# The chosen rows of a routed ffn: a gather by matmul against an indexed send through DRAM

## The chip, the core and the metric

The kernel runs on one core of a Trainium2 chip. Its time is the device time of one execution in microseconds (us); three executions of the kernel before are given. The engines are TensorE (PE, with its weight loads shown apart as PEld), VectorE (DVE), ScalarE (ACT), GpSimd (POOL) and SyncE (SP), which only issues transfers. All data are float32.

## What is computed

The input x has 64 samples of 256 rows and 256 columns. Two layers follow each other, each made of a graph attention block and an ffn block, and each block is added to what goes in. The change is in the ffn of layer 0, a routed one: every row gets a weight, the 127 rows of the greatest weight are taken out, go through a two-layer ffn, are scaled by their weight and are put back in their places.

```python
def _L0_ffn_ref(x, attention_mask, wr, br, w1, b1, w2, b2):
    weights = (jnp.einsum('bsd,do->bso', x, wr) + br)[..., 0]
    k = max(1, int(CAPACITY * s))
    kk = k - 1 if k > 1 else 1
    _, idx = jax.lax.top_k(weights, k)
    sel_idx = idx[:, :kk]
    sel = jnp.take_along_axis(x, sel_idx[:, :, None], axis=1)
    h = jax.nn.gelu(jnp.einsum('bkd,dh->bkh', sel, w1) + b1)
    y = jnp.einsum('bkh,hd->bkd', h, w2) + b2
    w_sel = jnp.take_along_axis(weights, sel_idx, axis=1)
    y = y * w_sel[..., None]
    batch_idx = jnp.arange(b)[:, None]
    processed = jnp.zeros_like(x).at[batch_idx, sel_idx].set(y)
    return processed + x
...
x = x + _L0_gnn_ref(_layernorm(x, axis=-1), ...)
x = x + _L0_ffn_ref(_layernorm(x, axis=-1), ...)
x = x + _L1_gnn_ref(_layernorm(x, axis=-1), ...)
x = x + _L1_ffn_ref(_layernorm(x, axis=-1), ...)
```

## The kernel before

The kernel works one sample at a time, but as a pipeline over samples. A sample's work is cut into some fifty steps, whose names begin with the block: `a_` and `b_` for the first attention block and its two stages, `q_` for the routed ffn, `g_` for the second attention block, `m_` for the last ffn (a Mamba block). The table STEPS gives each engine an order of steps, written out by hand, and each step has a lag: in turn t the engine does the step for sample t minus lag. All weights stay in SBUF. An engine does its steps strictly in the order of its list, and every step waits on semaphores for what it needs. There are 70 turns; in the first and the last few only some of the steps have a sample, the middle ones are one hardware loop in which every step has one.

A tile of 256 rows lies in SBUF as 128 partitions by two blocks (U = 2). The steps around the change, in the order in which a sample passes through them:

- `q_norm` (DVE, L819): the normalised rows `xn["q"]`.
- `q_route` (DVE, PE, ACT): the weight of each row, as a column `wcol` and as a row `wrow`.
- `q_rank` (DVE, L966): each row's rank is the number of rows with a greater weight (L971). From the ranks it makes `pick`, a matrix of 256 by 128 zeros and ones: a 1 where the row's rank is the slot's number (L978). Slot 127 holds -1, so only ranks 0 to 126 find a place.
- `q_gather` (PE, L1298): transposes `pick` into bank Q0 (two transposes, L1302, wanted later for the way out), and multiplies `xn["q"]` with `pick` (L1305), which gives the chosen rows already transposed. On ACT, `q_gather` copies both to SBUF as `pickT` and `selT` (L645, L646).
- `q_ffn1`, `q_gelu`, `q_ffn2` (PE, ACT, DVE), and `q_scatter` (PE, L1329), which puts the results back in their rows by a product with `pickT`.

On PE the steps `m_da`, `a_turn`, `g_att`, `b_pturn` stand just ahead of `q_gather`, and `b_att`, `m_cum_col`, `q_ffn1.0` just behind. `b_att` (L1284 with output A) needs `pT_b`, which ACT copies out of PSUM in its `b_pturn` (L608). ACT's own order there is `g_att` (L616, it waits for PE's `g_att`), `b_pturn` (L608), `g_elu` (L632), `q_gather` (L645, L646).

On POOL the step `m_dt_log` is a chain of thirteen tiny instructions (L458 to L470), each waiting for the one before, then `dt` (L478) and `m_da` (L483, L484). Its last instruction lets PE's `m_da` (L1379, the transposes of dA) go. SP issues in each turn the loads of two copies of a sample (L351, L360), the store of the result (L371), and a store and a spread of the cumulated sums through a DRAM scratch (L365, L367).

Of the kernel before, what the change touches and what calls it, by code (L numbers as in the profile page):

```python
# [7 lines left out]
ALU = mybir.AluOpType  # L8
ACT = mybir.ActivationFunctionType
F32 = mybir.dt.float32  # L10
I32 = mybir.dt.int32
AX_X = mybir.AxisListType.X

P = 128
# [30 lines left out]
def gnn_ffn_mamba_kernel(nc, x, adj, mlp1_w, mlp1_b, mlp2_w, mlp2_b, W_fc, a_fc, W_hand, a_hand,  # L45
# [24 lines left out]
    with ExitStack() as ctx:  # L70
        def sb(name, shape, dt=F32):
            return ctx.enter_context(nc.sbuf_tensor(name, shape, dt))
# [98 lines left out]
        pick = sb("pick", [P, U, P])  # L171
        pickT = sb("pickT", [P, N])
# [37 lines left out]
        cum_dram = nc.dram_tensor("cum_dram", [NH, N], F32, kind="Internal").ap()  # L210

# [8 lines left out]
        def rows1(half, u, extra=0):  # L220
# [13 lines left out]
            wsum_ready w_ps wrow_ready rank_ready pick_ready sel_ps sel_ready  # L234
# [11 lines left out]
        out_stored = sem("out_stored")  # L246

# [68 lines left out]
        def _(sp):  # L316
# [56 lines left out]
            turns(sp, "sync", dict(a_load=a_load, a_residual=a_residual, m_spread=m_spread, m_store=m_store), {})  # L373
# [4 lines left out]
        def _(pool):  # L378
            def constants():
# [34 lines left out]
                pool.wait_ge(PL, 5)  # L414

# [78 lines left out]
            def m_rms(b):  # L494
# [5 lines left out]
                q_turn=q_turn,  # L500
                m_turn=m_turn, m_dt_log=m_dt_log, m_da=m_da, m_xrow=m_xrow,
# [230 lines left out]
        def _(v):  # L732
# [233 lines left out]
            def q_rank(b):  # L966

                v.wait_ge(S["wrow_ready"], b)
                spare = gsq[:, :, :].rearrange("p (a c) r -> p a (c r)", a=4)
                for u in range(U):  # L970
                    last = nc.vector.scalar_tensor_tensor(out=spare[:, u, :], in0=wrow[:], scalar=wcol[:, u:u + 1],  # L971
                                                          in1=tie_gap[:, u, :], op0=ALU.subtract, op1=ALU.is_ge,
                                                          accum_out=rank[:, u:u + 1])
                last.then_inc(S["rank_ready"], 1)
                v.wait_ge(S["rank_ready"], b)

                for u in range(U):
                    last = nc.vector.tensor_scalar(pick[:, u, :], slot[:], rank[:, u:u + 1], None, ALU.is_equal)  # L978
                last.then_inc(S["pick_ready"], 1)
# [147 lines left out]
        def _(pe):  # L1127
# [341 lines left out]
```

## Time and profile before

| what | value |
|---|---|
| median of 3 executions | 3751.22 us (3750.86 to 3752.01) |
| the profiled execution, its own time | 3752.41 us |
| span of its profile, first to last instruction | 3750.7 us |
| PE busy | 3618.9 us, 96% |
| DVE busy | 2973.1 us, 79% |
| ACT busy | 2364.2 us, 63% |
| POOL busy | 993.9 us, 26% |
| mean granted clock of TensorE | 0.985 of 2.4 GHz |
| moved by DMA | 126.85 MB |

The span is the time between the first and the last instruction in the profile; 1.7 us of the execution lie around it. Busy time counts neither waits nor the issue of transfers. The ends of matmuls are modelled in the profile and overlap with the next matmul's start, so that PE's rows overlap in time, and a short wait of PE can hide under such an end. PEld shows when the weights (the stationary operand) of a matmul are loaded, which happens ahead of the matmul and needs the operand to be there. A float32 matmul of the program is two rows of the trace; a transpose is one.

### The profile page before, as it was taken

Reading aid. Unit: us, or ns where it says so; the run is one execution under the profiler, and the core shown is the slowest. Engines: PE = TensorE matmul, PEld = TensorE weight load, DVE = VectorE, ACT = ScalarE, POOL = GpSimd, SP = SyncE. Lnnn points to the kernel's source line nnn. Section 1 sums busy time; section 2 is a strip of 40 time slices with the busy share of each in tenths; the row PEclk is TensorE's granted clock in tenths of the full one; section 3 lists DMA queues with packets and bytes.
Section 4 is the critical chain, followed back from the end, with each engine's and each line's share of the span. In section 5 each row is a group of like instructions: output and inputs, shape, how many; then the busy total and the mean of one; then the engine's idle time right before and its main releaser. Section 6 shows DMA issues by size and latency. Waiting matters only on the chain.

```text
span 3750.7 us, 63924 instructions
## 1 busy us (share of the span) xinstructions
PE 3618.9 (96%) x21016; PEld 3158.1 (84%) x21016; DVE 2973.1 (79%) x7729; ACT 2364.2 (63%) x5314; POOL 993.9 (26%) x1821
## 2 busy tenths in 40 slices
PE   6799999999999999999999999999999999999975
PEld 4688888888888888888888888888888888888864
DVE  3468878878888888888888888888887887888875
ACT  2356666667666666666666666666666666666654
POOL 0022232232232232232222223223223223223222
PEclk8899999999999999999999999999999999999998
DMA  3000100100100110110010010010010010010000
GB/s 102 12 26 32 39 28 31 39 28 31 39 28 31 39 36 23 39 39 23 36 39 28 31 39 28 31 39 28 31 39 28 31 39 28 31 39 29 30 29 31
DMA packets 73763, 126.85 MB, mean 34 GB/s; under 512 B 9984, under 2 KB 64128, under 8 KB 65536
## 3 DMA queue, kind: packets, MB, share of 16 engines
q1 hardware_dynamic: 69360, 126.39, 9.8%
q10 hardware_dynamic: 4368, 0.03, 0.1%
q8 instruction: 18, 0.29, 0.0%
q14 instruction: 17, 0.14, 0.0%
HBM read 109.10 MB, written 17.30 MB: 34 GB/s over the span
## 4 chain that ended last, share of the span: by engine, by line
PE 87%; DVE 8%; issue 2%; ACT 1%; POOL 0%; ACTq 0%; DVEq 0%; POOLq 0%
PE A L1199 12%; PE M L1335 7%; PE A L1219 7%; PE Q L1323 6%; PE A L1237 6%; PE A L1188 6%; PE Q L1316 6%; PE M L1369 6%; PE M L1428 6%; PE A L1284 3%; PE A L1246 3%; PE Q L1246 3%; PE Q L1284 3%; PE A L1229 2%; PE M L1357 2%
## 5 line engine op out<-in xcount | busy, mean ns | idle before, releaser
L1199 PE MATMUL A<-w_fc,o1T 128*128 128x256 f32 (+1 forms) x2048 | 454.7, 380 | 3.8 <-ACT o1T L541 3.8
L1199 PEld LDWEIGHTS A<-w_fc,o1T 128*128 128x128 f32 x2048 | 382.9, 189 | 57.8 <-ACT o1T L541 4.0
L433 POOL TENSOR_TENSOR var_m<-mv_m,epsilon 128x2 f32<-128x2 f32 x64 | 12.6, 197 | 1414.7 <-DVE mv_m L813 1414.7
L710 ACT ACTIVATE dec<-cumB,cumcol 128x256 f32<-128x256 f32 (+1 forms) x1024 | 366.2, 443 | 0.0
L1022 DVE SCALAR_TENSOR_TENSOR acc<-M,w_conv,acc 128x255 f32<-128x255 f32 (+2 forms) x768 | 315.0, 470 | 0.0
L1335 PE MATMUL M<-xT_m,w_in 128*128 128x256 f32 x1280 | 297.5, 379 | 0.8 <-DVE tz L1064 0.5
L1219 PE MATMUL A<-h,low 128*128 128x257 f32 (+1 forms) x1024 | 256.4, 395 | 22.9 <-DVE low L854 14.0
L1335 PEld LDWEIGHTS M<-xT_m,w_in 128*128 128x128 f32 x1280 | 237.7, 190 | 32.1 <-DVE tz L1064 2.0
L1323 PE MATMUL Q<-w_down,gsq 128*128 128x256 f32 x1024 | 241.2, 390 | 9.7 <-DVE gsq L995 9.7
L1316 PE MATMUL Q<-selT,w_up 128*128 128x128 f32 x2048 | 249.5, 275 | 0.9 <-ACT selT L646 0.9
L1064 DVE SCALAR_TENSOR_TENSOR tz<-tz,M 128x512 f32<-128x512 f32 x128 | 88.1, 688 | 202.5 <-ACT tz L693 202.5
L1188 PE MATMUL A<-xT_a,w_mlp 128*128 128x256 f32 x1024 | 236.1, 384 | 8.3 <-ACT xT_a L533 5.1
L1237 PE MATMUL A<-e,w_mlp 128*128 128x256 f32 x1024 | 241.0, 389 | 0.7 <-DVE e L878 0.7
L1219 PEld LDWEIGHTS A<-h,low 128*128 128x128 f32 x1024 | 189.1, 194 | 61.5 <-DVE low L854 38.6
L1316 PEld LDWEIGHTS Q<-selT,w_up 128*128 128x128 f32 x2048 | 238.8, 192 | 1.2 <-ACT selT L646 1.1
L1428 PE MATMUL M<-w_comb,xr 128*128 128x256 f32 x1024 | 231.6, 379 | 3.4 <-DVE xr L1085 3.4
L1323 PEld LDWEIGHTS Q<-w_down,gsq 128*128 128x128 f32 x1024 | 193.5, 194 | 47.1 <-DVE gsq L995 22.2
L1369 PE MATMUL M<-xT_m,w_in 128*128 128x256 f32 x1024 | 231.7, 379 | 0.0
L658 ACT ACTIVATE acc<-M,c_conv,w_conv 128x256 f32<-128x256 f32 x320 | 168.4, 567 | 92.1 <-PE M L1335 92.1
L490 POOL TENSOR_TENSOR xdt<-xr,dt 128x1024 f32<-128x1024 f32 x64 | 129.4, 2022 | 366.2 <-ACT xr L699 366.2
L1072 DVE TENSOR_TENSOR dec<-dec,cb 128x2048 f32<-128x2048 f32 (+1 forms) x128 | 223.8, 1749 | 1.7 <-ACT dec L714 1.6
L1188 PEld LDWEIGHTS A<-xT_a,w_mlp 128*128 128x128 f32 x1024 | 192.6, 193 | 33.6 <-issue 9.0
(235 smaller groups left out, 8830.3 us busy)
## 6 DMA issues: line engine op xcount, KB each, us to landing
cumB<-cum_dram SPq DMA_DIRECT2D x64, 1024.0 KB, 4.7
x_in<-in_x SPq DMA_DIRECT2D x64, 256.0 KB, 2.8
x<-in_x SPq DMA_DIRECT2D x64, 256.0 KB, 2.9
out<-x3b SPq DMA_DIRECT2D x64, 256.0 KB, 2.8
w_mlp<-in_L_gnn_mlp_w SPq DMA_DIRECT2D x2, 512.0 KB, 6.3
w_fc<-in_L_gnn_W_fc SPq DMA_DIRECT2D x2, 512.0 KB, 8.6
w_up<-in_L_ffn_w SPq DMA_DIRECT2D x1, 1024.0 KB, 11.7
w_down<-in_L_ffn_w SPq DMA_DIRECT2D x1, 1024.0 KB, 12.9
```

The lines of the kernel that those rows point to most:

```text
L710: last = nc.scalar.activation(dec[:, h, :], columns[:, h, :], ACT.Relu, bias=cumcol[:, i, h:h + 1], scale=-1.0)
L1022: last = nc.vector.scalar_tensor_tensor(out=acc[:, k, late:], in0=src, scalar=w_conv[:, k, tap:tap + 1], in1=acc[:, k, late:], op0=ALU.mul ...
L1188: last = nc.tensor.matmul(ps[:, (m - m0) * N:(m - m0 + 1) * N], w_mlp1[:, k, m * P:(m + 1) * P], xT["a"][:, k, :], start=(k == 0), stop=(k ...
L1199: last = nc.tensor.matmul(rows1(half, u, 2), o1T[:, k, u * P:(u + 1) * P], w_fc[:, k, half, 0:D + 2 * i], start=(k == 0), stop=(k == KH - 1))
L1219: last = nc.tensor.matmul(rows1(half, u, 1), p1[:, j, u * P:(u + 1) * P], h1[:, j, half, 0:D + 1 - half], start=(j == 0), stop=(j == U - 1))
L1237: last = nc.tensor.matmul(A1[:, m * N:(m + 1) * N], w_mlp2[:, k, m * P:(m + 1) * P], z1T[:, k, :], start=(k == 0), stop=(k == KH - 1))
L1246: last = nc.tensor.matmul(banks[u][:, 0:D + 2], src[:, c, u * P:(u + 1) * P], w[:, c, :], start=(c == 0), stop=(c == KD - 1))
L1316: last = nc.tensor.matmul(ps[:, (m - m0) * P:(m - m0 + 1) * P], w_up[:, c, m * P:(m + 1) * P], selT[:, c, :], start=(c == 0), stop=(c == K ...
L1323: last = nc.tensor.matmul(Q0[:, 0:D], gl[:, m, :], w_down[:, m, :], start=(m == 0), stop=(m == KF - 1))
L1335: last = nc.tensor.matmul(ps[:, at:at + N], w_in[:, c, X0 + k * P:X0 + (k + 1) * P], xT["m"][:, c, :], start=(c == 0), stop=(c == KD - 1))
L1369: last = nc.tensor.matmul(ps[:, (k - 2 * i) * N:(k - 2 * i + 1) * N], w_in[:, c, Z0 + k * P:Z0 + (k + 1) * P], xT["m"][:, c, :], start=(c ...
L1428: last = nc.tensor.matmul(M2[:, u * D:(u + 1) * D], yg[:, c, u * P:(u + 1) * P], w_comb[:, c, :], start=(c == 0), stop=(c == KI - 1))
```

## The change

PE no longer multiplies with `pick` to gather. In its place:

- DVE computes `place` after the ranks, 128 by 2 whole numbers: the rank, plus one where the rank is 127 or more. Row 127 of the scratch is so never written by a sample.
- POOL sends `xn["q"]` to a DRAM scratch `sel_dram` of 257 rows, row by row to the row named by `place`. That is one indirect DMA for each of the two blocks, 128 rows of 1 KB each, in a new step `q_send`. It stands in the middle of `m_dt_log`, which is cut in two: its first two instructions before `q_send`, the other eleven behind.
- SP reads the first 128 rows of the scratch back into `sel` when both sends have landed, in a new step `q_sel` between `m_store` and `m_spread`.
- PE's `q_gather` keeps the two transposes of `pick`, waits for the read, and transposes `sel` (two transposes) where it had four matmuls.
- Once, at the start, POOL writes a row of zeros into row 127 of the scratch and waits for it.
- DVE's `q_norm` and `q_rank` each wait for the sends of the sample before.

```diff
-    "gpsimd": [('a_norm', 0), ('q_norm', 2), ('g_norm', 3), ('q_turn', 2), ('m_rms', 5), ('m_dt_log', 4), ('m_da', 4), ('m_turn', 4), ('m_norm', 3), ('m_xrow', 4)],
-    "sync": [('a_load', 0), ('a_residual', 2), ('m_store', 6), ('m_spread', 5)],
...
+    "gpsimd": [
+        ("a_norm", 0), ("q_norm", 2), ("g_norm", 3), ("q_turn", 2), ("m_rms", 5), ("m_dt_log.0", 4), ("q_send", 2),
+        ("m_dt_log.1", 4), ("m_da", 4), ("m_turn", 4), ("m_norm", 3), ("m_xrow", 4),
+    ],
+    "sync": [
+        ("a_load", 0), ("a_residual", 2), ("m_store", 6), ("q_sel", 3), ("m_spread", 5),
+    ],
...
+            def q_sel(b):
+
+                sp.wait_ge(sel_sent, 32 * b)
+                sp.dma_start(sel[:], sel_dram[0:P, :]).then_inc(sel_back, 16)
...
+                nc.gpsimd.dma_start(sel_dram[TOPK:TOPK + 1, :], tie_gap[0:1, 0, :]).then_inc(unused_row, 16)
+                pool.wait_ge(unused_row, 16)
...
+            def q_send(b):
+
+                after(S["place_ready"], b)
+                before(pool, S["sel_ps"], b)
+                pool.nop(nofuse=True)
+                for u in range(U):
+                    nc.gpsimd.indirect_dma_start(sel_dram, bass.IndirectOffsetOnAxis(place[:, u:u + 1], 0),
+                                                 xn["q"][:, u, :], None).then_inc(sel_sent, 16)
...
-                for i, link in enumerate(links):
+                for i in ((0, 1), range(2, CHAIN))[half]:
...
+                    if k == "q" and not (isinstance(b, int) and b < 2):
+                        v.wait_ge(sel_sent, 32 * (b - 1))
...
-
+                if not (isinstance(b, int) and b < 2):
+                    v.wait_ge(sel_sent, 32 * (b - 1))
+                nc.vector.scalar_tensor_tensor(out=place[:], in0=rank[:], scalar=float(TOPK), in1=rank[:], op0=ALU.is_ge,
+                                               op1=ALU.add).then_inc(S["place_ready"], 1)
...
+                pe.wait_ge(sel_back, 16 * b)
                 for c in range(KD):
-                    for u in range(U):
-                        last = nc.tensor.matmul(Q0[:, N + c * P:N + (c + 1) * P], xn["q"][:, u, c * P:(c + 1) * P],
-                                                pick[:, u, :], start=(u == 0), stop=(u == U - 1))
+                    last = nc.tensor.transpose(Q0[:, N + c * P:N + (c + 1) * P], sel[:, c * P:(c + 1) * P], ident[:])
                 last.then_inc(S["sel_ps"], 1)
```

The order of all other steps is the same. On PE, at the head of the hardware loop, `q_gather` stood like this before:

```order
L1273 MATMUL A<-ident,sc_b 128x128 x4
L295 UNCONDITIONAL_BRANCH
L295 ISA
L1302 MATMUL Q<-ident,pick 128x128 x2
L1305 MATMUL Q<-pick,xn_q 128x128 x4
L1280 REGISTER_ALU
L1284 MATMUL A<-hp_b,pT_b 128x256 x4
```

And it stands like this in the change, where lines further down in the file have moved by some fifty:

```order
L1331 MATMUL A<-ident,sc_b 128x128 x4
L329 UNCONDITIONAL_BRANCH
L329 ISA
L1360 MATMUL Q<-ident,pick 128x128 x2
L1361 REGISTER_ALU
L1363 MATMUL Q<-ident,sel 128x128 x2
L1338 REGISTER_ALU
L1342 MATMUL A<-hp_b,pT_b 128x256 x4
```

The four matmuls of L1305 have become two transposes of `sel`; the step before and the step behind are the same. On POOL, in the same loop, `m_dt_log` began like this before (`dt_w` are its small tiles):

```order
L458 TENSOR_TENSOR dt_w<-dt_e,twos 128x16
L475 ISA
L459 TENSOR_TENSOR dt_w<-dt_w,inverse 128x16
L475 REGISTER_ALU
L460 TENSOR_TENSOR dt_w<-dt_e,dt_w 128x16
```

And like this in the change:

```order
L509 TENSOR_TENSOR dt_w<-dt_e,twos 128x16
L526 ISA
L510 TENSOR_TENSOR dt_w<-dt_w,inverse 128x16
L491 DMA sel_dram<-xn_q,place 257x256 x2
L526 REGISTER_ALU
L511 TENSOR_TENSOR dt_w<-dt_e,dt_w 128x16
```

Two sends now stand behind the second instruction of the chain, and the eleven instructions behind them, `dt` and `m_da` follow only then. On SP the loop now issues as follows; the read of `sel` is the new row between the store of the result and the two transfers of the cumulated sums:

```order
L410 DMA out<-x3b 128x2x256
L405 REGISTER_ALU
L406 DMA sel<-sel_dram 128x256
L398 REGISTER_ALU
L399 DMA cum_dram<-cumT 8x256
L400 REGISTER_ALU
L401 DMA cumB<-cum_dram 128x2048
```

Nothing else of SP's order has moved.

## Rows read from the trace of the kernel before

**Rows 1.** The page, busy time by engine and the chain that ended last

```profile
PE 3618.9 (96%) x21016; PEld 3158.1 (84%) x21016; DVE 2973.1 (79%) x7729; ACT 2364.2 (63%) x5314; POOL 993.9 (26%) x1821
...
PE 87%; DVE 8%; issue 2%; ACT 1%; POOL 0%; ACTq 0%; DVEq 0%; POOLq 0%
```

**Rows 2.** One turn in the middle: stretch, length, busy us (count), clock, DMA

```profile
2018.60:2074.40 55.80, 55.65 (x330) 48.81 (x328) 46.10 (x121) 36.87 (x84) 15.43 (x28) 1.00 0.10 33
```

**Rows 3.** Timeline of PE around q_gather: start us, length us, instruction, count

```profile
2015.33 1.89 PE L1284 MATMUL Q<-hp_g,pT_g 128*128 128x256 f32 x8
...
2017.50 0.38 PE L1302 MATMUL Q<-ident,pick 128*128 128x128 f32 x2
2017.72 1.06 PE L1305 MATMUL Q<-pick,xn_q 128*128 128x128 f32 x8
2018.64 1.99 PE L1284 MATMUL A<-hp_b,pT_b 128*128 128x256 f32 x8
```

**Rows 4.** Timeline of the weight loads in the same place

```profile
2014.46 0.30 PEld L1379 LDWEIGHTS M<-ident,dA 128*8 128x8 f32 x2
...
2017.61 0.97 PEld L1305 LDWEIGHTS Q<-pick,xn_q 128*128 128x128 f32 x8
2018.63 0.73 PEld L1284 LDWEIGHTS A<-hp_b,pT_b 128*128 128x128 f32 x4
```

**Rows 5.** Timeline of ACT there; in brackets the idle time before and its end

```profile
2017.26 0.84 ACT L616 ACTIVATE ea_g<-Q,rr_g 128x256 f32<-128x256 f32 x2 [0.39 <-PE Q L1284]
2017.99 0.59 ACT L608 COPY pT_b<-A 128x512 f32<-128x512 f32 x1
```

**Rows 6.** Timeline of DVE: the end of q_rank and what follows

```profile
2004.44 0.48 DVE L978 TENSOR_SCALAR pick<-slot,rank 128x128 f32<-128x128 f32 x2
2007.06 0.69 DVE L1064 SCALAR_TENSOR_TENSOR tz<-tz,M 128x512 f32<-128x512 f32 x1 [2.14 <-ACT tz L693]
```

**Rows 7.** Timeline of POOL in that turn

```profile
2002.67 2.91 POOL L459 TENSOR_TENSOR dt_w<-dt_w,inverse 128x16 f32<-128x16 f32 x1
...
2009.45 0.26 POOL L484 TENSOR_SCALAR dt<-dt 128x16 f32<-128x16 f32 x1
2009.68 1.27 POOL L448 TENSOR_TENSOR x3b<-x,c_lin 128x512 f32<-128x512 f32 x1
```

**Rows 8.** Timeline of SP in that turn, the store of the sums

```profile
2016.14 0.30 SPq L365 DMA_DIRECT2D cum_dram<-cumT  x1
```

**Rows 9.** The page, DMA issues: count, KB each, median us to landing

```profile
cumB<-cum_dram SPq DMA_DIRECT2D x64, 1024.0 KB, 4.7
x_in<-in_x SPq DMA_DIRECT2D x64, 256.0 KB, 2.8
```

**Rows 10.** Timeline of the start: issues of transfers and the first sample

```profile
3.05 1.44 ACTq L512 DMA_DIRECT2D c_conv<-in_L_ffn_conv_b  x1
...
5.77 0.20 POOL L433 TENSOR_TENSOR var_a<-mv_a,epsilon 128x2 f32<-128x2 f32 x1
...
7.68 1.09 PE L1177 MATMUL A<-ident,xn_a 128*128 128x128 f32 x4 [7.68 <-DVE xn_a L821]
...
11.88 1.28 ACT L533 ACT_TABLE_LOAD   x1 [11.88 <-issue]
12.10 4.34 SPq L335 DMA_DIRECT2D w_route<-in_L_ffn_wr  x1
```

**Rows 11.** Timeline of the first sample's gather

```profile
119.38 1.83 PEld L1305 LDWEIGHTS Q<-pick,xn_q 128*128 128x128 f32 x8
119.41 0.59 ACT L608 COPY pT_b<-A 128x512 f32<-128x512 f32 x1 [1.21 <-PE A L1273]
...
121.09 1.73 PEld L1284 LDWEIGHTS A<-hp_b,pT_b 128*128 128x128 f32 x8
```

**Rows 12.** Timeline of the last turn with a q_gather, POOL and PE

```profile
3627.09 0.26 POOL L484 TENSOR_SCALAR dt<-dt 128x16 f32<-128x16 f32 x1
...
3627.40 0.38 PE L1379 MATMUL M<-ident,dA 128*8 128x128 f32 x2
```

More of the change, by code:

```diff
@@ L11 @@
 I32 = mybir.dt.int32
+U32 = mybir.dt.uint32
 AX_X = mybir.AxisListType.X
@@ L29 @@
 STEPS = {
-    "tensor": [('q_gather', 3), ('b_att', 2), ('m_cum_col', 5), ('q_ffn1.0', 3), ('b_res', 2), ('q_ffn1.1', 3), ('a_mlp1.0', 1), ('a_mlp1.1', 1), ('m_xrow', 5), ('m_cb', 5), ('a_fc.0', 1), ('a_fc.1', 1), ('q_ffn2', 3), ('a_bcast', 1), ('m_turn', 4), ('q_scatter', 3), ('m_y.0', 5), ('m_y.1', 5), ('a_att.0', 1), ('g_turn', 3), ('a_att.1', 1), ('g_proj', 3), ('m_out', 5), ('g_bcast', 3), ('m_ss', 5), ('a_uturn', 1), ('m_dt', 4), ('q_route', 2), ('a_mlp2', 1), ('m_z', 4), ('g_pturn', 3), ('b_proj', 1), ('m_xbc_a', 4), ('b_bcast', 1), ('m_xbc_b', 4), ('m_da', 4), ('a_turn', 0), ('g_att', 3), ('b_pturn', 1)],
@@ L32 @@
-    "scalar": [('a_att', 1), ('m_gated', 5), ('a_elu_b', 1), ('g_proj', 3), ('q_route', 2), ('m_dt_exp', 4), ('g_exp', 3), ('a_mlp2', 1), ('m_z', 4), ('b_proj', 1), ('g_pturn', 3), ('m_xbc_a', 4), ('m_xbc_b', 4), ('b_exp', 1), ('g_att', 3), ('b_pturn', 1), ('g_elu', 3), ('q_gather', 2), ('b_att', 1), ('b_elu_b', 1), ('a_turn', 0), ('m_silu', 4), ('q_gelu_a', 2), ('a_mlp1', 0), ('m_decay.0', 4), ('q_gelu_c', 2), ('m_decay.1', 4), ('m_xrow', 4), ('a_factors', 0), ('a_fcol', 0), ('g_turn', 2), ('m_turn', 3)],
@@ L33 @@
-    "gpsimd": [('a_norm', 0), ('q_norm', 2), ('g_norm', 3), ('q_turn', 2), ('m_rms', 5), ('m_dt_log', 4), ('m_da', 4), ('m_turn', 4), ('m_norm', 3), ('m_xrow', 4)],
-    "sync": [('a_load', 0), ('a_residual', 2), ('m_store', 6), ('m_spread', 5)],
+    "tensor": [
+        ("q_gather", 3), ("b_att", 2), ("m_cum_col", 5), ("q_ffn1.0", 3), ("b_res", 2), ("q_ffn1.1", 3),
+        ("a_mlp1.0", 1), ("a_mlp1.1", 1), ("m_xrow", 5), ("m_cb", 5), ("a_fc.0", 1), ("a_fc.1", 1), ("q_ffn2", 3),
+        ("a_bcast", 1), ("m_turn", 4), ("q_scatter", 3), ("m_y.0", 5), ("m_y.1", 5), ("a_att.0", 1), ("g_turn", 3),
+        ("a_att.1", 1), ("g_proj", 3), ("m_out", 5), ("g_bcast", 3), ("m_ss", 5), ("a_uturn", 1), ("m_dt", 4),
+        ("q_route", 2), ("a_mlp2", 1), ("m_z", 4), ("g_pturn", 3), ("b_proj", 1), ("m_xbc_a", 4), ("b_bcast", 1),
+        ("m_xbc_b", 4), ("m_da", 4), ("a_turn", 0), ("g_att", 3), ("b_pturn", 1),
+    ],
@@ new lines @@
+    "vector": [
+        ("g_stats", 4), ("a_probs", 2), ("g_norm", 4), ("m_y.0", 6), ("a_att", 2), ("m_y.1", 6), ("q_norm", 3),
+        ("g_proj", 4), ("m_sq", 6), ("q_route", 3), ("a_elu_c", 2), ("g_mask", 4), ("m_ms", 6), ("a_uturn", 2),
+        ("g_lrelu", 4), ("m_dt", 5), ("a_norm", 1), ("g_max", 4), ("m_out", 6), ("q_rank", 3), ("m_gate", 5),
+        ("b_proj", 2), ("b_mask", 2), ("b_lrelu", 2), ("b_max", 2), ("g_pturn", 4), ("m_scan", 5), ("m_conv_b.0", 5),
+        ("b_pturn", 2), ("m_conv_b.1", 5), ("g_elu_b", 4), ("m_conv_b.2", 5), ("m_cum_col", 5), ("b_elu_c", 2),
+        ("b_x1", 2), ("q_gelu_a", 3), ("m_silu", 5), ("g_x3", 4), ("q_stats", 2), ("a_stats", 0), ("q_gelu_b", 3),
+        ("m_stats", 4), ("m_cb", 5), ("a_fc", 1), ("m_norm", 4), ("q_ffn2", 3), ("m_mix.0", 5), ("a_fcol", 1),
+        ("m_mix.1", 5), ("q_scatter", 3), ("a_maxima", 1), ("q_x2", 3),
+    ],
@@ new lines @@
+    "scalar": [
+        ("a_att", 1), ("m_gated", 5), ("a_elu_b", 1), ("g_proj", 3), ("q_route", 2), ("m_dt_exp", 4), ("g_exp", 3),
+        ("a_mlp2", 1), ("m_z", 4), ("b_proj", 1), ("g_pturn", 3), ("m_xbc_a", 4), ("m_xbc_b", 4), ("b_exp", 1),
+        ("g_att", 3), ("b_pturn", 1), ("g_elu", 3), ("q_gather", 2), ("b_att", 1), ("b_elu_b", 1), ("a_turn", 0),
+        ("m_silu", 4), ("q_gelu_a", 2), ("a_mlp1", 0), ("m_decay.0", 4), ("q_gelu_c", 2), ("m_decay.1", 4),
+        ("m_xrow", 4), ("a_factors", 0), ("a_fcol", 0), ("g_turn", 2), ("m_turn", 3),
+    ],
@@ L35 @@
+    "gpsimd": [
+        ("a_norm", 0), ("q_norm", 2), ("g_norm", 3), ("q_turn", 2), ("m_rms", 5), ("m_dt_log.0", 4), ("q_send", 2),
+        ("m_dt_log.1", 4), ("m_da", 4), ("m_turn", 4), ("m_norm", 3), ("m_xrow", 4),
+    ],
+    "sync": [
+        ("a_load", 0), ("a_residual", 2), ("m_store", 6), ("q_sel", 3), ("m_spread", 5),
+    ],
 }
@@ L171, in gnn_ffn_mamba_kernel @@
         pick = sb("pick", [P, U, P])
+        place = sb("place", [P, U], U32)
+        sel = sb("sel", [P, D])
         pickT = sb("pickT", [P, N])
@@ L210, in gnn_ffn_mamba_kernel @@
         cum_dram = nc.dram_tensor("cum_dram", [NH, N], F32, kind="Internal").ap()
+        sel_dram = nc.dram_tensor("sel_dram", [N + 1, D], F32, kind="Internal").ap()
         A0, A1, A2 = bank("A0"), bank("A1"), bank("A2")
@@ L246, in gnn_ffn_mamba_kernel @@
         out_stored = sem("out_stored")
+        sel_sent = sem("sel_sent")
+        sel_back = sem("sel_back")
+        unused_row = sem("unused_row")
         DV, PL, PEs, AC = [sem(f"setup{i}") for i in range(4)]
@@ L371, in m_store @@
                 sp.dma_start(out[b - 1].rearrange("(u p) d -> p u d", p=P), x4[:]).then_inc(out_stored, 16)
-            turns(sp, "sync", dict(a_load=a_load, a_residual=a_residual, m_spread=m_spread, m_store=m_store), {})
+            turns(sp, "sync", dict(a_load=a_load, a_residual=a_residual, m_spread=m_spread, q_sel=q_sel, m_store=m_store), {})
             sp.wait_ge(cum_stored, 16 * B)
@@ L451, in _, with m_dt_log @@
             CHAIN = 13
-            def m_dt_log(b):
-                after(S["dt_e_ready"], b)
+            def m_dt_log(b, half):
+                if half == 0:
+                    after(S["dt_e_ready"], b)
                 w = dt_w
@@ L472, in m_dt_log @@
                 assert len(links) == CHAIN
-                for i, link in enumerate(links):
+                for i in ((0, 1), range(2, CHAIN))[half]:
                     if i:
                         pool.wait_ge(S["dt_chain"], nth(b, CHAIN, i))
-                    link().then_inc(S["dt_chain"], 1)
+                    links[i]().then_inc(S["dt_chain"], 1)
+                if half == 0:
+                    return
                 after(S["dt_chain"], b * CHAIN)
@@ L499, in _ @@
                 a_norm=rstd_of("a"), q_norm=rstd_of("q"), g_norm=rstd_of("g"), m_norm=rstd_of("m"),
-                q_turn=q_turn,
-                m_turn=m_turn, m_dt_log=m_dt_log, m_da=m_da, m_xrow=m_xrow,
+                q_turn=q_turn, q_send=q_send,
+                m_turn=m_turn, **parts("m_dt_log", m_dt_log, 2), m_da=m_da, m_xrow=m_xrow,
                 m_rms=m_rms), dict(a_norm=constants, m_turn=first_m_turn, m_da=first_m_da))
```

3 lines of the change are left out of this document (1 added, 2 removed).

## The prediction

> **What bounds the kernel now.** I read the page first. PE is busy 96% of the span and 87% of the chain that ended last is PE's [rows 1]. One turn in the middle takes 55.80 us, PE is busy 55.65 us of it at a granted clock of 1.00 (2.4 GHz), DVE 46.10, ACT 36.87 and POOL 15.43 [rows 2]. By this view whatever is taken from PE comes off the time, and the change takes something from PE.
>
> The second view is the timeline around the step that changes. PE starts the transposes of `pick` at 2017.50, the gather's matmuls at 2017.72 and `b_att` at 2018.64 [rows 3]. PE's rows show no idle time there, but matmul ends are modelled: the gather's eight rows are given as 1.06 us and overlap `b_att`. So the third view is that of the weight loads. The eight of the gather take 0.97 us from 2017.61, the last one ending at 2018.58, and loads follow each other about 0.11 us apart ((2018.58 - 0.19 - 2017.61) / 7, where 0.19 is the length of one). The next would be due near 2018.50. The first of `b_att` starts at 2018.63 [rows 4]: it is held by about 0.13 us. What holds it is in the fourth view. ACT waits for PE's `g_att`, which ends at 2015.33 + 1.89 = 2017.22 [rows 3], works on `ea_g` from 2017.26, starts the copy `pT_b` at 2017.99 and ends it at 2017.99 + 0.59 = 2018.58 [rows 5]. `b_att` needs `pT_b`, and its load starts 0.05 us after that copy's end. **The start of `b_att` is thus set by `g_att` and two pieces of ACT's work, 1.41 us after `g_att`'s end, and not by the gather that stands between.** The reader is to see that a busy PE row covers this, and that the weight load gives it away.
>
> **What the change removes.** The four matmuls are eight rows from 2017.72 to 2018.64: 0.92 us, 0.115 each [rows 3]. In their place stand two transposes, priced by the two of `pick`: 2017.50 to 2017.72, 0.22 us [rows 3]. That is 0.70 us less work of PE in each of 64 turns, 45 us. But in the middle turns PE comes to `b_att` 0.70 us sooner and waits until 2018.63 as before, since neither `g_att`, `ea_g` nor `pT_b` has moved. The 0.13 us of waiting becomes 0.83, the turn stays 55.80, and the gain is 0. Behind `b_att` nothing is sooner, for PE is in order. The clock: 0.8 us of idle in 55.80 leaves PE busy 98%; I put nothing for it.
>
> In the first sample it is otherwise. The weight loads of the gather run from 119.38 to 121.09, 1.71 us at the lower clock of that stretch (0.21 each); `pT_b` is ready at 119.41 + 0.59 = 120.00 [rows 11]. Two transposes take 0.43 in place of 1.71, so `b_att` could start 1.28 sooner, at 119.81, and is held until 120.05: I put a gain of 1.2 us with the tail of the pipeline. The other turns at the ends can give at most 0.70 each; I put 0.
>
> **What the change adds: the sends on POOL.** The trace has no DMA issued by POOL. Call G the time for which the two sends hold POOL. They stand behind the second instruction of the chain, which ends at 2002.67 + 2.91 = 2005.58 [rows 7]; `place` is there by then (`pick` starts at 2004.44 [rows 6], and `place` stands ahead of it). Queued behind them are eleven links, `dt` and `m_da`, which end at 2009.45 + 0.26 = 2009.71 [rows 7] and would end at 2009.71 + G. PE's `m_da` waits for them; its first weight load starts at 2014.46 [rows 4]. The cover is 4.75 us, and PE's work ahead (`m_z`, `m_xbc`) is what gives it. Up to G = 4.75 the sends cost nothing; beyond, `m_da` is late, `g_att` behind it is late by the same, and so is `b_att`: each us over costs one us in each of about 60 turns. `x3b`, further back on POOL, ends at 2010.95 [rows 7] and is wanted only by the next turn's `m_out`.
>
> G from below: two issues at 0.30, the shortest row of SP, 0.60 [rows 8]. From above: two at 4.34, the longest issue in the trace, 8.7 [rows 10]. I take two at 1.44, G = 2.9: the row of a load of many small pieces on ACT's queue [rows 10], nearest in kind to 128 rows with an address each.
>
> In the last turn with a gather the cover is gone: `dA` is ready at 3627.09 + 0.26 = 3627.35 and PE's `m_da` starts at 3627.40 [rows 12], so there the cost is G - 0.05 = 2.85 us, once (0.55 to 8.65).
>
> **The way through DRAM.** The sends leave POOL at 2005.58 + 2.9 = 2008.5. A send carries 128 KB and the read brings 128 KB back. Loads of 256 KB land 2.8 us after their issue, of 1024 KB 4.7 [rows 9]; I take 2.8 each for the last send and the read: 2008.5 + 5.6 = 2014.1. PE asks for `sel` at 2017.72 [rows 3], and since `b_att` is held anyway, a `sel` at 2018.4 still costs nothing. The cover is 3.6 to 4.3 us; with 4.7 twice it is 2017.9, still in time. In the last turn the sends start at 3623.2 (POOL's chain ends 4.13 us before `dA`) and `sel` is back at 3631.7, while PE asks at about 3632.4, since `m_da` is late by 2.85: nothing more.
>
> **Further waits.** SP's wait for the sends blocks the store of the sums, at 2016.14 [rows 8], 5 us after it would end (2011.3). On DVE `place` is a short instruction ahead of `pick`, and DVE idles 2.14 us behind it [rows 6]: 0. DVE's waits for the sends of the sample before look back a turn: 0. At the start POOL waits for one row to reach DRAM, from 5.77 on [rows 10], 2.8 us by the loads. The first sample's transposes, 7.68 to 8.77, would end 2.8 later, at 11.6, but ACT can't copy them before its table load ends at 11.88 + 1.28 = 13.16 [rows 10]: 0, with a cover of 4.4 us. If the first send of a run takes longer than the cover, I allow 3 us.
>
> **The sum** against the profiled execution: 3752.41 + 0 (middle turns) - 1.2 (first sample) + 2.85 (last turn) = 3754.1. The median of the runs is 1.19 below that execution: 3752.9, say 3753. Its own bounds: G = 0.60 and 0.70 at two turns of the ends give 3751.2 + 0.55 - 1.2 - 1.4 = 3749; G = 4.75 and 3 us at the start give 3751.2 + 4.7 - 1.2 + 3 = 3758. A measurement of this kernel can tell about 0.2%, 7.5 us, from no change.
>
> **The rivals.** *PE is the bound at this place and each turn gets shorter.* For it: the chain is 87% PE's, and PE shows 0.15 us idle a turn [rows 1, 2]. Against it: the weight load that starts 0.05 us behind `pT_b` [rows 4, 5]. It would give 62 middle turns x 0.70 = 43.4 less: 3753 - 43 = 3710. Chance 0.10.
>
> *The sends are longer than their cover* (the other side). The place is PE's `m_da`, the point from which it decides G = 4.75. With two sends of 3 us, G = 6, it gives 60 x 1.25 = 75, and 3 more in the last turn: 3831. For it: nothing in the trace shows what such a send costs, and POOL needs 2.91 us for one power of 16 columns [rows 7]. Against it: the middle of the issue rows is half of the cover. Chance 0.18, most of it between 3759 and 3831.
>
> *POOL works through the indices one after the other*, so that a send costs as much as the longest issue, 4.34 [rows 10]: G = 8.7, 60 x 3.95 = 237, and 5.8 more in the last turn, 3996 or more. POOL's power, 0.18 us a column by 2.91 / 16 [rows 7], shows that its software can be as slow. Chance 0.05. The Trainium skill has a rule for this, GPSIMD Engine Reference, section Performance pitfalls for Q7 kernels: a small read command, such as one per gather index, costs about 102 cycles that don't overlap. At the 1.2 GHz of its section Specifications, an estimate from that page is 128 x 102 cycles = 10.9 us a send, and the sum by it would be over 4700; no row here shows it.
>
> *The rows come back late.* Landings of more than 4.7 us each put `sel` behind 2018.4; each us over costs about 62. At 5.7 each it is 3753 + 62 x 1.5 = 3846. Chance 0.03.
>
> **Chances.** Forecast, no change that can be told, 0.64; faster 0.10; the three slower ones 0.26. The forecast's own range is 3749 to 3758. To leave out no more than 0.2 (the faster rival, the one index after the other, the late landing and the far end of the long sends) the range reaches to G = 6: 3749 to 3831.
>
> **What the new profile would show.** Right: a turn of 55.80, the first weight load of `b_att` 0.05 us behind `pT_b`'s end and over 0.7 us behind the load before it, PE's `m_da` where it was before `g_att`, the read of `sel` landed before PE's transposes of `pick`, and a later `m_da` only in the last turn. Wrong: PE waiting for `dt` or dA on POOL in every turn (the sends are too long), PE waiting for `sel` (the way is), or a turn near 55.1 (the hold by `pT_b` isn't one).

## The result and the profile after

| what | before | with the change |
|---|---|---|
| median of 20 executions each, side by side | 3752.11 us (3749.96 to 3753.18) | 3758.82 us (3756.01 to 3761.78) |
| ratio | | 1.0019, 95% interval 1.0012 to 1.0026 |
| the profiled execution | 3752.41 us | 3761.53 us |
| its span | 3750.7 us | 3759.8 us |

The change made the kernel 6.7 us slower. That is under the 7.5 us which the prediction took as the limit of what can be told, but the interval of the ratio lies above 1, so the small loss is real. The forecast was 3753. The profiled execution lies 2.7 us above its median, so of the 9.1 us by which the two spans differ some belongs to that one execution.

The page of the kernel after, against [rows 1]:

```profile
PE 3589.2 (95%) x20632; PEld 3114.3 (83%) x20632; DVE 2977.2 (79%) x7793; ACT 2364.9 (63%) x5314; POOL 1124.7 (30%) x1950
PE 84%; DVE 9%; issue 3%; ACT 3%; POOL 1%; DMA 0%; DVEq 0%; POOLq 0%
```

PE has 29.7 us less to do and POOL 130.8 us more, and neither shows in the time. One middle turn, from `b_att` to `b_att`, against [rows 2]:

```profile
2020.72:2076.52 55.80, 55.12 (x323) 48.08 (x323) 46.17 (x122) 36.89 (x84) 17.45 (x30) 1.00 0.11 38
```

The length is the same, 55.80, with PE busy 0.53 us less. The weight loads at the place of the change, against [rows 4], and then ACT, against [rows 5] (L1342 was L1284, L661 was L608, L669 was L616):

```profile
2019.48 0.25 PEld L1360 LDWEIGHTS Q<-ident,pick 128*128 128x128 f32 x2
2019.70 0.25 PEld L1363 LDWEIGHTS Q<-ident,sel 128*128 128x128 f32 x2
2020.72 1.59 PEld L1342 LDWEIGHTS A<-hp_b,pT_b 128*128 128x128 f32 x8 [0.77 <-ACT pT_b L661]
```

```profile
2019.36 0.84 ACT L669 ACTIVATE ea_g<-Q,rr_g 128x256 f32<-128x256 f32 x2 [0.39 <-PE Q L1342]
2020.09 0.59 ACT L661 COPY pT_b<-A 128x512 f32<-128x512 f32 x1
```

`pT_b` ends at 2020.68, the load of `b_att` follows 0.04 us later, and what were 0.13 us of hidden waiting are now 0.77, with a releaser named. The chain that was read out of three views before stands in one row now, because the gather no longer covers it. Summed over the kernel, in the view of all waits (total us, times, longest):

```profile
PEld A L1342 <- ACT pT_b L661: 48.5, 64, 1.1
```

POOL in the same turn, against [rows 7], and SP's read of `sel`:

```profile
2004.76 2.91 POOL L510 TENSOR_TENSOR dt_w<-dt_w,inverse 128x16 f32<-128x16 f32 x1
2007.86 1.07 POOL L491 DMA_INDIRECT sel_dram<-xn_q,place  x1 [0.18 <-issue]
2009.23 0.97 POOL L491 DMA_INDIRECT sel_dram<-xn_q,place  x1 [0.30 <-issue]
2010.23 0.23 POOL L511 TENSOR_TENSOR dt_w<-dt_e,dt_w 128x16 f32<-128x16 f32 x1
...
2014.02 0.26 POOL L537 TENSOR_SCALAR dt<-dt 128x16 f32<-128x16 f32 x1
```

```profile
2011.65 0.34 SPq L406 DMA_DIRECT2D sel<-sel_dram  x1
```

From the end of L510 (2007.67) to L511 are 2.56 us where the chain's links stand 0.07 to 0.08 apart: G is 2.5 us (2.9 forecast). POOL ends at 2014.28, and the first load of PE's `m_da` starts at 2016.56: 2.28 of the 4.75 us of cover are left. The page gives the two ways through DRAM, in KB where known and median us to landing:

```profile
sel<-sel_dram SPq DMA_DIRECT2D x64, 128.0 KB, 2.0
sel_dram<-xn_q,place POOLq DMA_INDIRECT x128, 2.5
```

`sel` is back at 2011.65 + 2.0 = 2013.65, and PE asks at 2019.8.

**Where the 9.1 us are.** I put the two traces beside each other by the start of the two `pick` transposes, once in each sample. The changed kernel is 2.69 us late at the first one, 2.28 two turns on. Over the middle turns it makes up 0.3 (55.794 a turn for 55.800), then loses 1.1 in one turn, 3.96 in the last turn with a gather, and 2.05 behind it: 2.69 - 0.41 - 0.3 + 1.1 + 3.96 + 2.05 = 9.1.

*The start*, against [rows 10], on POOL, on the chain that ended last, and the first sample's copy on ACT:

```profile
6.01 0.77 POOL L454 DMA_DIRECT2D sel_dram<-tie_gap  x1 [0.31 <-POOL slot L452]
12.39 0.20 POOL L474 TENSOR_TENSOR var_a<-mv_a,epsilon 128x2 f32<-128x2 f32 x1 [5.61 <-DMA sel_dram<-tie_gap]
```

```profile
6.01 6.29 DMA sel_dram<-tie_gap
```

```profile
15.42 0.59 ACT L586 COPY xT_a<-A 128x512 f32<-128x512 f32 x1 [2.44 <-PE A L1235]
```

One row of 1 KB took 6.29 us to land, not 2.8. The first sample's statistics stand behind it, its transposes on PE start at 14.30 for 7.68, 6.62 later. ACT's table load covered the first 4.4: the copy starts at 15.42 for 13.17, 2.25 later. The other 0.4 us come behind the copy. One part has a row, PE's wait for `low`, a preparation that DVE does behind the second sample's statistics; these start at 20.68 for 13.18, because the second load of `x_in` went out only when the first sample's rows were read:

```profile
27.49 3.75 PE L1257 MATMUL A<-w_fc,o1T 128*128 128x258 f32 x16 [0.24 <-DVE low L796]
```

The rest differs from one execution to the next. The copy is 2.08 to 2.34 us later in each of the five kernels with this wait, but their sixteen matmuls of `a_mlp1` behind it take 5.41 to 6.38 us. The kernel of "The sends alone" below, whose steps are those of the changed kernel up to the first gather, has that gather at 120.21, where the changed kernel has 121.85.

*The last turn with a gather*, against [rows 12]. PE:

```profile
3632.77 0.49 PE L1436 MATMUL M<-ident,dA 128*8 128x128 f32 x2 [2.58 <-POOL dt L537]
3633.05 3.51 PE L1342 MATMUL Q<-hp_g,pT_g 128*128 128x256 f32 x8
```

PE waits 2.58 us for POOL, and `g_att` behind it takes 3.51 us for the 1.89 of [rows 3]. The windows show why (the columns of [rows 2]):

```profile
3633.05:3636.40 3.35, 3.35 (x10) 2.55 (x9) 3.07 (x8) 0.00 (x0) 0.90 (x1) 0.51 0.12 27
3640.00:3700.00 60.00, 38.22 (x198) 31.20 (x196) 39.00 (x84) 32.53 (x67) 13.34 (x25) 0.81 0.07 23
```

The granted clock is 0.51, the lower level of 1.2 GHz, right behind that idle stretch. In the drain it is 0.81 from 3640 to 3700; the kernel before has 0.88 in the 60 us at the same distance behind its last gather. This second difference does not follow from the stop. Four kernels have the same last turn, with PE idle for 2.58 or 2.59 us and `g_att` at 3.41 to 3.57. In the changed kernel and in that of "The sends alone" the drain runs at 0.81, and the tail, from the last gather to the end, takes 123.4 and 123.3 us. In the one with the zero row waited for later and in the one of "Moving PE's waiting work" the drain runs at 0.87 and the tail takes 120.6 and 120.9, less than the 121.34 of the kernel before. What sets the clock of the drain is open, and so is what the 2.05 us are due to.

*The one longer turn* (56.90 us). POOL, then PE:

```profile
3235.35 1.07 POOL L491 DMA_INDIRECT sel_dram<-xn_q,place  x1 [0.18 <-issue]
3239.72 0.98 POOL L491 DMA_INDIRECT sel_dram<-xn_q,place  x1 [3.30 <-issue]
```

```profile
3245.38 0.38 PE L1436 MATMUL M<-ident,dA 128*8 128x128 f32 x2 [0.95 <-POOL dt L537]
```

Between the two sends are 3.30 us of issue, 0.30 elsewhere. G is 5.5 there, over the cover of 4.75, and one link of the chain takes 0.69 for 0.22; PE waits 0.95. The gap stands between the 113th and the 114th send of the kernel.

### The profile page after: what moved, and what is told of

Same layout as the page of the kernel before. It is cut to its first block, busy times and chain, and to the rows that moved or that the text cites. A ratio compares the mean times of both kernels' runs of the same rounds, so it can differ in the third digit from the quotient of the medians.

```text
span 3759.8 us, 63718 instructions
## 1 busy us (share of the span) xinstructions
PE 3589.2 (95%) x20632; PEld 3114.3 (83%) x20632; DVE 2977.2 (79%) x7793; ACT 2364.9 (63%) x5314; POOL 1124.7 (30%) x1950
## 4 chain that ended last, share of the span: by engine, by line
PE 84%; DVE 9%; issue 3%; ACT 3%; POOL 1%; DMA 0%; DVEq 0%; POOLq 0%
PE A L1257 12%; PE M L1392 7%; PE A L1277 6%; PE Q L1380 6%; PE A L1295 6%; PE Q L1373 6%; PE A L1246 6%; PE M L1426 6%; PE M L1485 6%; PE A L1342 3%; PE A L1304 3%; PE Q L1342 3%; PE Q L1304 3%; PE A L1287 2%; PE M L1414 1%
## 5 line engine op out<-in xcount | busy, mean ns | idle before, releaser
L1485 PEld LDWEIGHTS M<-w_comb,xr 128*128 128x128 f32 x1024 | 194.0, 190 | 30.7 <-DVE xr L1143 3.9
```

The costliest lines, as they stand in the source:

```text
L1485: last = nc.tensor.matmul(M2[:, u * D:(u + 1) * D], yg[:, c, u * P:(u + 1) * P], w_comb[:, c, :], start=(c == 0), stop=(c == KI - 1))
```

## The experiments

Each ran beside the kernel before, whose medians were 3751.28, 3751.63 and 3751.88 in the three sets. "Turn" is the median distance of two gathers in the trace. Theory A, the prediction's: `b_att` is held by `pT_b`, so that PE's saved time is lost, and the sends hide in their cover. The rivals: PE is the bound, or the sends are paid in every turn. What two kernels of different sets differ by is told from their medians as they stand; the medians of the kernel before differ by up to 0.8 us between the sets (that of the result had 3752.11).

### PE's part alone

The kernel before, with two transposes in place of the four matmuls and nothing sent. They transpose half of `xn["q"]` instead of choosing rows.

```diff
-                    for u in range(U):
-                        last = nc.tensor.matmul(..., xn["q"][:, u, c * P:(c + 1) * P], pick[:, u, :], ...)
+                    last = nc.tensor.transpose(..., xn["q"][:, 0, c * P:(c + 1) * P], ident[:])
```

> The kernel before, in which PE's gather is cut to the two transposes of the change (of a block of the normalised rows, so the rows that reach the ffn are not the chosen ones); no sends, no scratch, no read. Held by pT_b: the middle turn stays 55.80 us, b_att's first weight load starts 0.05 us behind pT_b's end, and the time is that of before less about 1 us of the first sample, 3751. PE is the bound there: 62 turns of 55.10, 3709.

Measured: 3751.45 (3750.1 to 3752.67), ratio 0.9999 (0.999 to 1.0008), turn 55.79.

```profile
2017.78 1.59 PEld L1284 LDWEIGHTS A<-hp_b,pT_b 128*128 128x128 f32 x8 [0.77 <-ACT pT_b L608]
```

The saved 0.70 us are gone without any send or wait for `sel`. The rival that PE is the bound here is refuted.

### The sends alone

The changed kernel with everything sent and read back, but PE gathers by its four matmuls, behind the wait for `sel`.

> The changed kernel with all its sends, reads and waits, in which PE gathers by its four matmuls as before. Held by pT_b: PE's 0.70 us are free in a middle turn, the turn is 55.80, and the time is that of the change plus 0.6 us of the first sample, 3759. PE is the bound and the sends ate its gain: 62 x 0.70 us more than the change, 3802.

Measured: 3760.36 (3758.93 to 3762.25), ratio 1.0023 (1.0014 to 1.0032), turn 55.79. The loss of the change is that of the sends and the start; none of it is a loss in every turn.

### Twice as many sends

Each send is done a second time, to a scratch that nobody reads, and the waits for the sends count twice as far.

```diff
                     nc.gpsimd.indirect_dma_start(sel_dram, ..., xn["q"][:, u, :], None).then_inc(sel_sent, 16)
+                    nc.gpsimd.indirect_dma_start(spare_dram, ..., xn["q"][:, u, :], None).then_inc(sel_sent, 16)
```

> The changed kernel with each send done twice, the second time to another scratch that nobody reads. Cover by PE's m_da: the sends hold POOL 5.1 us in place of 2.5, dA is ready 0.3 us behind the time at which PE wants it, 0.3 to 0.4 us in each of 60 turns and 2.6 in the last: 3780 to 3785, with PE waiting for POOL in every turn. If POOL's time is hidden whatever it is: 3759 to 3762. If each us of POOL costs a us of the turn: 3915.

Measured: 3799.59 (3798.61 to 3800.95), ratio 1.013 (1.0114 to 1.0145), turn 56.30. POOL is held 5.0 us. The PE row of a middle turn:

```profile
2036.39 0.38 PE L1439 MATMUL M<-ident,dA 128*8 128x128 f32 x2 [0.35 <-POOL dt L540]
```

The cover ends where the prediction put it: 0.25 us beyond 4.75, and POOL's `dA` took 0.59 where it takes 0.22 else, together 0.6, and the turn is 0.50 longer. That is 30 us. The rest over the expectation are two odd turns (60.66 and 61.97 for 56.30, 10 us) and the last turn (55.28 for 49.53, 5.8; the expectation allowed 2.6 for it). Both odd turns have the long gap:

```profile
1689.16 0.98 POOL L494 DMA_INDIRECT spare_dram<-xn_q,place  x1 [3.30 <-issue]
...
3271.16 0.96 POOL L492 DMA_INDIRECT sel_dram<-xn_q,place  x1 [3.27 <-issue]
```

The first stands behind the 113th send, the second behind the 226th. In each of the nine kernels with two sends a turn there is one such gap, behind the 113th send, at 3225 to 3240 us; here the same count is reached at 1689. So the gap goes by the number of sends and not by the turn or the time. What POOL does in it no row shows.

### The ends: the zero row, the last turn

```diff
-                pool.wait_ge(unused_row, 16)
...
+                if isinstance(b, int) and b == 1:
+                    pool.wait_ge(unused_row, 16)
```

The wait moves from the start to the first sends, some 100 us later.

> The changed kernel, in which POOL waits for the row of zeros only ahead of the first send and not before the first sample. The wait at the start is what the first turns lost: the first gather comes 2.7 us or a little more sooner, and the time is 3 us below the change, 3756. If something else of the send's first use costs the time (code, the first indirect send): 3759, the loss only moves.

Measured: 3754.68 (3753.6 to 3759.16), ratio 1.0011 (1.0002 to 1.002). The first gather is at 117.01 (121.85 in the changed kernel, 119.16 before), so more than the 2.69 comes back. The wait is not what the other 2.15 are due to: the first sample's copy on ACT starts at 13.07, as before the change, and the sixteen matmuls of `a_mlp1` behind it take 5.12 us for 6.18. Why they do is open.

In the second kernel the last sample neither sends nor reads, and PE gathers by matmul for it:

```diff
+                if isinstance(b, int) and b == B:
+                    return
```

> The changed kernel, in which the last sample alone is gathered by the four matmuls as before, with no send and no read for it. If the last turn's loss is POOL's sends ahead of the chain for dA: that turn is 49.5 us as before in place of 53.5, the clock doesn't fall behind it, and the time is 4 to 6 us below the change, 3753 to 3755. If the loss is the way through DRAM or the tail's own: 3759.

Measured: 3754.31 (3753.26 to 3755.54), ratio 1.0007 (0.9998 to 1.0016); last turn 49.34, tail 121.17. PE no longer waits there, and the matmuls keep the upper clock:

```profile
3629.67 1.89 PE L1346 MATMUL Q<-hp_g,pT_g 128*128 128x256 f32 x8
```

Each end is worth some 4 us by the medians, 4.1 and 4.5 (3.3 and 4.0 if each is taken against the kernel before of its own set). For the last turn that is what the turn itself gives, 4.15 us. Then both in one kernel:

> The changed kernel with both losses at the ends taken out: the wait for the zero row stands ahead of the first sends, and the last turn gathers by matmul without sends. Middle turns 55.79, first gather near 117.1, last turn 49.5 and no lower clock behind it. From the changed kernel's 3758.8 this takes 4.1 and 4.5 us: 3750 to 3751. If the two losses share a cause or one is made up in the drain, 3753 or more.

Measured: 3753.30 (3750.27 to 3759.31), ratio 1.0005 (0.9996 to 1.0014). Together they gave 5.5, not 8.6. In the profiled execution the last turn is 50.26 and the tail 122.41, 2.2 over the last kernel, which is of the size of the shortfall. Two windows of 40 us in the drain, of this kernel and then of the one before it, whose last gather is 2.2 us later:

```profile
3640.00:3680.00 40.00, 30.23 (x152) 24.14 (x150) 23.17 (x54) 18.14 (x40) 12.36 (x23) 0.85 0.05 19
```

```profile
3640.00:3680.00 40.00, 30.86 (x162) 24.77 (x160) 23.76 (x53) 19.84 (x45) 12.40 (x23) 0.91 0.02 8
```

The granted clock is 0.85 for 0.91. PE had not stopped ahead of the last gather in either, so here too the clock of the drain differs without such a stop. What decides it was not isolated, and so a microsecond or two of each end stays open.

### Moving PE's waiting work ahead of b_att

If `b_att` is held 0.77 us and PE has other work ready, the work can fill the hold: `m_cum_col` (2 transposes) and `b_res` (4) are 0.66 us. In the changed kernel:

```diff
-        ("q_gather", 3), ("b_att", 2), ("m_cum_col", 5), ("q_ffn1.0", 3), ("b_res", 2), ("q_ffn1.1", 3),
+        ("q_gather", 3), ("b_res", 2), ("m_cum_col", 5), ("b_att", 2), ("q_ffn1.0", 3), ("q_ffn1.1", 3),
```

> The changed kernel, in which PE does the residual's transposes (b_res, 0.44 us) and those of the sums (m_cum_col, 0.22 us) ahead of b_att in place of behind it. Held by pT_b: 0.66 of the 0.83 us in which PE waits are filled, the middle turn becomes 55.14, and the time is 40 us below that of the change, 3719. If the wait ahead of b_att is not on the path that sets the turn: 3759, as the change.

Measured: 3757.66 (3756.51 to 3759.03), ratio 1.0017 (1.0008 to 1.0026), turn 55.78. A miss by 39 us. The hold before `b_att` is filled, and another has opened 6 us on; PEld, then DVE:

```profile
2018.44 1.59 PEld L1342 LDWEIGHTS A<-hp_b,pT_b 128*128 128x128 f32 x8
2020.06 3.76 PEld L1373 LDWEIGHTS Q<-selT,w_up 128*128 128x128 f32 x32
2024.39 1.59 PEld L1246 LDWEIGHTS A<-xT_a,w_mlp 128*128 128x128 f32 x8 [0.58 <-issue]
```

```profile
2023.59 0.69 DVE L997 SCALAR_TENSOR_TENSOR ue_b<-A,ue_b 128x512 f32<-128x512 f32 x1
```

The DVE instruction ends at 2024.28, PE's load follows 0.12 behind. The same on the kernel before, and, with both repairs of the ends, on the changed one:

> The kernel before with the same two steps moved ahead of b_att. Held by pT_b: only the 0.13 us of holding can be filled, the middle turn becomes 55.67, 8 us less than before, 3744. If the new order gives its gain by itself and not by filling a wait: as much as in the changed kernel, 40 us, 3712.

> The changed kernel with three edits: b_res and m_cum_col ahead of b_att, the wait for the row of zeros only ahead of the first send, the last sample gathered by matmuls. If the three causes are separate: 40 + 3 + 5 us below the change, 3711, a ratio of 0.989 to before. If the turn's gain is lost elsewhere: 3751.

Measured: 3786.25 (3785.53 to 3786.77), ratio 1.0093 (1.0078 to 1.0109), turn 56.31; and 3752.22 (3750.68 to 3753.19), ratio 1.0002 (0.9993 to 1.0011), turn 55.78.

### The two moves of ACT's and PE's steps

On the kernel with both ends repaired, ACT copies `pT_b` ahead of `ea_g`:

```diff
-("g_att", 3), ("b_pturn", 1), ("g_elu", 3)
+("b_pturn", 1), ("g_att", 3), ("g_elu", 3)
```

> The same, and ACT does b_pturn ahead of g_att, so that pT_b no longer waits for the two pieces of ea_g. Theory A (behind b_att the chain of ACT and DVE through ea_b and ue_b is a second hold with about 0.1 us free): b_att starts sooner, a_mlp1 waits for ue_b instead, a turn of 55.7, 3744 or no change at all. Rival B (b_att was the only hold): 0.3 us a turn, 55.5, 3733.

Measured: 3741.54 (3740.91 to 3743.18), ratio 0.9973 (0.9963 to 0.9984), turn 55.60. PEld, then DVE:

```profile
2011.13 1.59 PEld L1347 LDWEIGHTS A<-hp_b,pT_b 128*128 128x128 f32 x8 [0.48 <-ACT pT_b L666]
...
2017.17 3.32 PEld L1251 LDWEIGHTS A<-xT_a,w_mlp 128*128 128x128 f32 x16
```

```profile
2016.37 0.69 DVE L1002 SCALAR_TENSOR_TENSOR ue_b<-A,ue_b 128x512 f32<-128x512 f32 x1
```

Neither size was right: 0.20 us a turn, not 0.1 and not 0.29. The wait for `pT_b` is 0.29 shorter (0.77 to 0.48), but from `b_att`'s load to that of `a_mlp1` there are now 6.04 us for 5.95 in the kernel with the same ends, and `a_mlp1` follows `ue_b` by 0.11: 0.09 has gone over to the second hold, explained below. Then also `g_pturn` behind `b_bcast` (PE) and behind `m_xbc_a` (ACT):

```diff
-("m_z", 4), ("g_pturn", 3), ("b_proj", 1), ("m_xbc_a", 4), ("b_bcast", 1)
+("m_z", 4), ("b_proj", 1), ("m_xbc_a", 4), ("b_bcast", 1), ("g_pturn", 3)
```

> The same, and g_pturn stands behind b_bcast on PE and behind m_xbc_a on ACT, so that b_bcast, the head of DVE's gapless stretch, starts sooner. Theory A (ACT's and DVE's chain from b_bcast to ue_b bounds the turn, and PE's saved 0.7 us is worth something only when that chain begins sooner): 55.5 a turn, about 3733. If DVE's total work from the scan on bounds the turn, whatever its head, 3750. If g_pturn becomes late for g_att, slower than 3751.

> The two moves of steps alone on the kernel before, with the gather by four matmuls. Here PE reaches b_att 0.7 us later, with 0.13 us to spare before, so the matmuls bound b_att at once: at most 0.13 a turn, 3743 to 3752. If it gains as much as the changed kernel with the same moves, that gain has nothing to do with the change.

Measured: 3738.89 (3736.34 to 3741.34), ratio 0.9965 (0.9951 to 0.9978), turn 55.56, with the change; 3744.92 (3744.32 to 3746.81), ratio 0.9983 (0.9974 to 0.9992), turn 55.67, without it. Of the forecast 0.3 a turn 0.24 came with the change, and the 0.13 that the matmuls leave came exactly without it. The weight loads of the latter:

```profile
2011.99 0.25 PEld L1302 LDWEIGHTS Q<-ident,pick 128*128 128x128 f32 x2
...
2013.10 1.60 PEld L1284 LDWEIGHTS A<-hp_b,pT_b 128*128 128x128 f32 x8
```

ACT's copy ended at 12.88 there, and `b_att`'s load comes 0.22 behind it with no wait: now the gather is the bound at this place. So the change is worth 0.11 us a turn, 6.0 us in all, where ACT's copy is ready before the matmuls are through, and nothing where it is not. What bounds the turn of 55.56 is open: there the load of `a_mlp1` comes 0.17 behind `ue_b`, later than a hold by it would have it. The kernel with the change, both ends and both moves is the fastest of all, 0.35% under the kernel before.

## Why the prediction was right, and where it was off

**The hold by `pT_b`** was right, by its place and its size: 0.77 us of waiting for 0.83, the load 0.04 us behind the copy's end for 0.05, and the gain 0. PE's part alone shows it without the rest of the change, and the kernels in which ACT copies `pT_b` sooner show it from the other side. The loss that was measured has nothing to do with it: all of it lies at the ends and in one odd turn, in terms that the prediction had put too low.

**That nothing but this hold stood there** was not said in the prediction, but I took it for granted in the expectations after it, and there it failed by 39, 42 and 41 us. `a_mlp1` writes the bank (A in the rows) that DVE's step `b_x1` reads last (L942, with `ue_b`), and `ue_b` comes from `b_att` through three pieces of ACT (`ea_b`). In the kernel before, DVE and then PEld:

```profile
2023.78 0.69 DVE L942 SCALAR_TENSOR_TENSOR ue_b<-A,ue_b 128x512 f32<-128x512 f32 x1
```

```profile
2022.80 1.86 PEld L1316 LDWEIGHTS Q<-selT,w_up 128*128 128x128 f32 x16
2024.59 1.60 PEld L1188 LDWEIGHTS A<-xT_a,w_mlp 128*128 128x128 f32 x8
```

L942 ends at 2024.47 and the load of `a_mlp1` starts 0.12 us behind. It is 0.11 to 0.12 too where PE waits by name for `ue_b` (2024.39 for 2024.28 in the one above). So the second hold was already touched before, though the loads of L1316 and L1188 stand there 0.11 apart, as loads without a wait do, and no wait is written. From `b_att`'s load PE's own work brings it to `a_mlp1` after 5.95 us, and the way through ACT and DVE after 5.84 + 0.12 = 5.96: equal. Whoever moves 0.66 us ahead of `b_att` leaves PE 5.3 us behind it and waits for `ue_b`. With the change that is neutral, since the hold of 0.77 only changes its place; in the kernel before only 0.13 are free in front, `b_att` comes 0.53 later, and the turn grew by 0.51.

**The sends** were right: G 2.5 for 2.9, with a cover of 4.75 that four sends confirmed. The Trainium skill's rule on one read command per gather index (GPSIMD Engine Reference, Performance pitfalls for Q7 kernels) made 10.9 us a send as an estimate; the trace shows 1.0 for 128 rows, so this kind of send does not fall under it. What the prediction did not hold is an issue gap of 3.30 us behind the 113th send, which costs 1.1 us.

**The landing** was right by its effect, 2.5 and 2.0 us for 2.8 each. The Trainium skill fits a transfer issued by GpSimd as 2.0 us and bytes over 436,000 a microsecond (DMA: Bandwidth & Descriptors, Anatomy of one DMA); for 128 KB that is 2.3 by estimate, and the trace agrees within 0.2. For the first one, 1 KB, it would be 2.0, and the trace shows 6.29: the measurement decides.

**The start**, put at 0 with 3 us allowed, is the first term that was mis-sized. The mechanism and the cover of 4.4 were as told; the landing was 6.29 for 2.8, which makes 2.25 at ACT's copy. 2.69 was lost at the first gather, of which 0.4 is DVE's `low` and what differs between executions.

**The first sample**, put at a gain of 1.2, is another. The prediction's own rows gave 1.04 (121.09 - 120.05), and the rest had no source. `b_att`'s load gained 1.05 (122.73 for 121.09, 1.64 late instead of 2.69), but its loads then took 2.20 us at a lower clock for 1.73, and 0.4 was left two turns on. In PE's part alone nothing was left: its first two turns between gathers are 0.2 us longer than before.

**The last turn**, put at 2.85, is the third: 3.96. The wait itself was 2.58. The rest is the clock that fell behind it and made `g_att` 1.62 us longer. The prediction had put the clock at nothing for 0.8 us in a turn (rightly so there) and never asked for a wait of 2.6. The 2.05 us behind the last gather are no part of this: the kernel with the zero row waited for later has the same last turn and none of them.

The sum with what was measured, 2.28 + 1.1 - 0.3 + 3.96 + 2.05, is 9.1 for the forecast 1.65. Without the 2.05 it is 7.0, and the median moved by 6.7. It ended 0.8 above the forecast's own range of 3749 to 3758, and well inside the wider one, which reached to 3831 for sends that turned out short. So the middle turns were foreseen by their mechanism, and the ends only by their place.

## What to carry to other kernels

A busy engine's saving counts only up to the next thing that it waits for, and modelled matmul ends hide such a wait: compare the start of the first weight load with the end of what produces its operand. Behind the first hold look for the second, by adding up the other engines' chain between two of PE's steps, before moving work into the gap. What an indexed send hides in the middle is paid in full where the pipeline runs empty: keep the first transfer of an engine off the start's chain, and let the last sample go the old way.

## What the runs showed of the hardware

- An indexed send of 128 rows of 1 KB holds POOL for 1.0 us (966 to 1105 ns over 128 of them), four in a row start 1.26 to 1.41 us apart, and it lands 2.5 us after its issue (2.4 to 3.4).
- POOL's first transfer, one row of 1 KB, landed 6.29 us after its issue (6.1 to 6.4 in the ten kernels with it).
- The gap between two sends was 3.3 us behind the 113th send of a kernel, and 0.30 else. It stands there in all ten kernels with sends, and with four sends a turn again behind the 226th. It made a turn of two sends 1.0 to 1.1 us longer, and the two turns of four sends 4.4 and 5.7. What POOL does there no row shows.
- PE idle for 2.58 us in the last turn was followed by a granted clock of 0.51 and 3.51 us for work that takes 1.89 at 1.00. In the five kernels with such a stop there (2.6 to 3.4 us) it was 0.50 to 0.55. PE idle of 0.5 to 0.8 us in each of 60 turns left the clock at 1.00.
- The granted clock of the drain, 60 us behind the last gather, was 0.81 or 0.87 in kernels with the same stop ahead of it, and a drain at 0.81 took 2.4 to 2.8 us longer.
